# Ten groups of payload scatters moved from the moments stage into the last ticks of the ranking stage of a graph network kernel

## The chip, the cores and the metric

The kernel runs on one core of one Trainium2 chip. The metric is the device time of one execution in microseconds. The kernel before takes 5331.2 us, the median of three runs (5328.56, 5331.2 and 5365.31 us). The execution that the profiler recorded took 5342.85 us, with a profiled span of 5341.1 us.

## The reference

Four graph layers run over 50000 nodes of 128 features and 25000 edges (padded to 25600 = 200 tiles of 128), each inside `x = layernorm(x + layer(x))`. The two stages that matter here belong to the first layer and to the preparation of the second:

```
def _L0_gnn_ref(x, W, b, gamma, beta, edge_index):
    xw = x @ W
    src = jnp.concatenate([edge_index[0], loops]); dst = jnp.concatenate([edge_index[1], loops])
    deg = jax.ops.segment_sum(ones, dst, num_segments=N)
    dinv = jnp.where(deg > 0, jax.lax.rsqrt(deg), 0.0)
    msg = xw[src] * (dinv[src] * dinv[dst])[:, None]
    h = jax.ops.segment_sum(msg, dst, num_segments=N) + b
    mean = jnp.mean(h, axis=0); var = jnp.mean(jnp.square(h - mean), axis=0)
    h = jax.nn.relu((h - mean) * jax.lax.rsqrt(var + BN_EPS) * gamma + beta)
    return x + h
```

The second layer groups edges by their source, `row = edge_index[0]`. The edges come sorted by destination, so the kernel itself works out, for each edge, its place in the order by source (its rank), and writes the edge's record of four integers to that place of a table in DRAM.

## The kernel before, in words

The kernel is a row of stages, each a block of one instruction stream per engine. A stage begins on all engines only when the stage before has ended on all of them. The four stages of interest, in order:

- **Counting** (`count_phase`, L218) makes histograms of the nodes. Beside it GpSimd (POOL) gathers the source rows of `x` for the first FG = 10 groups of edges (`fetch_sources`, L208).
- **Ranking and summing** (`rank_and_sum_phase`, L348) handles T = 200 tiles of 128 edges, in EG = 50 groups of GT = 4 tiles. For each tile VectorE (DVE) makes one-hot rows (`hots`), counts equal sources inside the tile (`twins`, first half of the rank, `parts[:, 0]`) and picks the count of earlier tiles (`picks`, second half, `parts[:, 1]`). TensorE (PE) and ScalarE (ACT) look up tables, weigh the gathered rows and sum them by destination. ACT copies the sums of a tile to `rank_sums`, a ring of US = 3 groups (`copy_sums`), and POOL scatters them to the table `agg` in DRAM. One pass of POOL's `pipeline` is called a tick here: in tick m it gathers the source rows of group m + 10 (four indirect DMAs, L213) while m < 40, and then scatters the sums of group m - 3 (four indirect DMAs, L423), which waits for `copied`. ACT, before it copies a group's sums, waits until the scatter of three groups earlier has landed. After all 200 tiles one DVE instruction adds the two halves to `rank`, an integer table of 128 x 200 (L489).
- **Moments** (`moments_phase`, L1308) goes over the node table in NG + 1 = 49 blocks of 1024 rows: SP loads a block of `x` and of `agg`, DVE combines them in three instructions (L1383, L1388, L1395), PE sums products (L1440, which counts up `used` once a block), SP stores the block. A short chain of small steps on DVE, PE and ACT ends with `gcn_c` (L1421). Beside it POOL runs `send_payloads` (L1501): 50 groups of four indirect DMAs, each of which writes the records of one tile of 128 edges to `sorted4` at their ranks. Group g waits until the payload group two before has landed, and until `used` has reached g - 1.
- **Order by source** (`order_phase` with the tag ord_s, L574) loads `sorted4`, first of all by SP (L593).

POOL's queue is strictly in order: an instruction that waits holds up all behind it.

Of the kernel before, what the change touches and what calls it, by code (L numbers as in the profile page):

```python
# [16 lines left out]
ALU = mybir.AluOpType  # L17
# [9 lines left out]
T = 200  # L27
# [5 lines left out]
GT = 4  # L33
EG = T // GT
# [168 lines left out]


FG = 10


def fetch_sources(k, rows, g):  # L208
# [139 lines left out]
def rank_and_sum_phase(k, order, rows):  # L348

    nc = k.nc  # L350
    with ExitStack() as st:
# [34 lines left out]
        with nc.Block(no_gpsimd_drain=True) as block:  # L386
# [25 lines left out]
            def _(pool):  # L412
                nc.gpsimd.iota(eid[:, :], pattern=[[P, T]], base=0, channel_multiplier=1).then_inc(s["numbered"], 1)

                def gather(g):
                    if g + FG < EG:
                        fetch_sources(k, rows, g + FG)

                def scatter(g):
                    pool.wait_ge(s["copied"], (g + 1) * GT)  # L420
                    for j in range(GT):
                        t = g * GT + j
                        nc.gpsimd.indirect_dma_start(  # L423
                            out=k.agg, out_offset=bass.IndirectOffsetOnAxis(ap=order.last_idx[:, t:t + 1], axis=0),
                            in_=sums[:, g % US, j, :], in_offset=None, bounds_check=N - 1, oob_is_err=False)\
                            .then_inc(k.scattered[g % US], 16)

                pipeline(EG, (gather, 0), (scatter, 3))
                for g in range(EG - US, EG):
                    pool.wait_ge(k.scattered[g % US], stored(g))  # L430

# [1 line left out]
            def _(dve):  # L433
# [49 lines left out]
                    nc.vector.tensor_tensor(cross[:, u, :, :], dst_b[:, u, :, :], prev,  # L483
                                            ALU.is_equal).then_inc(s["masked"], 1)

                pipeline(T, (hots, 0), (twins, 0), (picks, 2), (masks, 2))
                dve.wait_ge(s["twinned"], T)
                dve.wait_ge(s["rank_picked"], T)
                nc.vector.tensor_tensor(rank[:, :], parts[:, 0, :], parts[:, 1, :], ALU.add).then_inc(s["ranked"], 1)  # L489
                dve.wait_ge(s["ranked"], 1)  # L490

            @block.scalar
            def _(act):
# [1004 lines left out]
CS = 4  # L1498


def send_payloads(k, pool, used):  # L1501

    def sent(g):
        return k.scatter_base[RF + g % 2] + g // 2 * 16 * GT + 16 * GT

    for g in range(EG):
        if g >= 2:
            pool.wait_ge(k.scattered[RF + g % 2], sent(g - 2))
            pool.wait_ge(used, min(g - 1, NG + 1))
        for t in range(g * GT, (g + 1) * GT):  # L1510
            k.nc.gpsimd.indirect_dma_start(  # L1511
                out=k.sorted4[:, :], out_offset=bass.IndirectOffsetOnAxis(ap=k.rank[:, t:t + 1], axis=0),
                in_=k.payload[:, t, :], in_offset=None).then_inc(k.scattered[RF + g % 2], 16)
    for g in range(EG - 2, EG):
        pool.wait_ge(k.scattered[RF + g % 2], sent(g))
    for g in range(EG):
        k.scatter_base[RF + g % 2] += 16 * GT

# [1886 lines left out]
```

## Time and profile before

| What | us |
|---|---|
| median of the runs | 5331.2 |
| the profiled execution | 5342.85 |
| its span | 5341.1 |
| busy: PE / DVE / POOL / ACT | 3358.2 / 3813.6 / 3005.8 / 2396.5 |
| ranking stage, first to last scatter of POOL | 191.1 to 684.7 |
| moments stage, first instruction | 687.8 |
| payload scatters of POOL, first and last start | 688.4 and 982.4 |
| first instruction of the order by source | 985.37 |

Times are microseconds from the start of the span unless marked ns. Busy time of an engine is the time in its instructions; register, semaphore and DMA-issuing instructions of the hardware queues are not in it, but POOL's indirect DMAs are, since POOL itself makes their descriptors. The idle time before an instruction is put down to what released it ("issue" means to nothing that the profile shows).

### The profile page before, as it was taken

Reading aid. Unit: us, or ns where it says so; the run is one execution under the profiler, and the core shown is the slowest. Engines: PE = TensorE matmul, PEld = TensorE weight load, DVE = VectorE, ACT = ScalarE, POOL = GpSimd, SP = SyncE. Lnnn points to the kernel's source line nnn. Section 1 sums busy time; section 2 is a strip of 40 time slices with the busy share of each in tenths; the row PEclk is TensorE's granted clock in tenths of the full one; section 3 lists DMA queues with packets and bytes.
Section 4 is the critical chain, followed back from the end, with each engine's and each line's share of the span. In section 5 each row is a group of like instructions: output and inputs, shape, how many; then the busy total and the mean of one; then the engine's idle time right before and its main releaser. Section 6 shows DMA issues by size and latency. Waiting matters only on the chain. (4 is left out here: it accounts for less than half of the span.)

```text
span 5341.1 us, 70175 instructions
## 1 busy us (share of the span) xinstructions
PE 3358.2 (63%) x19808; PEld 2649.4 (50%) x19808; DVE 3813.6 (71%) x10966; ACT 2396.5 (45%) x5571; POOL 3005.8 (56%) x2733
## 2 busy tenths in 40 slices
PE   6888855288612367643277644556999993774453
PEld 1455554277601255533266633334777763764443
DVE  8877777399834467622377777886899874877997
ACT  6444400299700156532123213544666662325776
POOL 7777577245577433257777726765776556107400
PEclk9989977699855689865588867878999996996666
DMA  5666588299757778832367527883555545876654
GB/s 208 180 190 198 167 304 289 92 299 314 242 187 260 249 237 276 275 107 73 96 212 259 186 61 224 279 277 118 182 192 187 178 142 161 264 218 227 232 213 155
DMA packets 684358, 1095.92 MB, mean 205 GB/s; under 512 B 108888, under 2 KB 451979, under 8 KB 677722
## 3 DMA queue, kind: packets, MB, share of 16 engines
q1 hardware_dynamic: 580772, 908.27, 51.9%
q0 software_dynamic: 103200, 183.16, 11.4%
q8 instruction: 162, 2.65, 0.2%
q14 instruction: 224, 1.84, 0.1%
HBM read 664.33 MB, written 439.19 MB: 207 GB/s over the span
## 5 line engine op out<-in xcount | busy, mean ns | idle before, releaser
L2242 PE MATMUL ro_end<-vals,end_mask 128*2 128x128 f32 x1600 | 240.5, 315 | 373.2 <-DVE vals L2106 276.4
L2368 POOL DMA_INDIRECT sc_rows<-layer,node_idx x400 | 391.5, 979 | 124.4 <-issue 121.6
L719 POOL DMA_INDIRECT agg<-late_agg_sent,d_last x200 | 223.2, 1116 | 324.5 <-issue 295.8
L2242 PEld LDWEIGHTS ro_end<-vals,end_mask 128*2 128x2 f32 x1600 | 147.3, 96 | 457.2 <-DVE vals L2106 287.6
L2974 ACT ACTIVATE tf_hidden<-tf_h_ps,pre_b 128x512 f32<-128x512 f32 x392 | 268.8, 687 | 227.0 <-PE tf_h_ps L3014 217.0
L2268 PE MATMUL ro_acc<-vals,ro_mask 128*126 128x128 f32 x1600 | 248.3, 320 | 187.3 <-ACT ro_square L2200 140.5
L1601 POOL DMA_INDIRECT cap_own<-layer,w_own x200 | 205.7, 1028 | 278.9 <-SPq L1581 227.2
L3026 PE MATMUL tf_o_ps<-pre_w,tf_hidden 128*128 128x128 f32 (+1 forms) x3136 | 358.0, 275 | 0.0
L3026 PEld LDWEIGHTS tf_o_ps<-pre_w,tf_hidden 128*128 128x128 f32 (+1 forms) x3136 | 353.9, 192 | 0.5 <-issue 0.5
L3014 PE MATMUL tf_h_ps<-tf_x_t,pre_w 128*128 128x512 f32 x784 | 348.2, 597 | 9.5 <-ACT tf_hidden L2974 8.3
L213 POOL DMA_INDIRECT x_src<-in_x_dram,node_idx x200 | 295.6, 1478 | 81.7 <-issue 59.4
L2056 POOL TENSOR_TENSOR vals<-ro_both,ro_weight 126x1024 f32<-126x1024 f32 x75 | 144.9, 1932 | 341.2 <-ACT ro_weight L2224 300.5
L2268 PEld LDWEIGHTS ro_acc<-vals,ro_mask 128*126 128x126 f32 x1600 | 229.5, 230 | 210.3 <-issue 174.9
L1104 PE MATMUL ml_conv_out<-pre_mean_wt,ml_conv_tsb 128*128 128x128 f32 (+1 forms) x784 | 178.2, 420 | 241.6 <-DVEq L3206 228.7
L791 POOL DMA_INDIRECT msg_rows<-values,s_eid x200 | 206.9, 1034 | 186.5 <-POOLq L71 100.9
L1104 PEld LDWEIGHTS ml_conv_out<-pre_mean_wt,ml_conv_tsb 128*128 128x128 f32 (+1 forms) x784 | 166.4, 322 | 254.0 <-ACT ml_conv_tsb L1090 180.2
L872 PE MATMUL msg_acc<-msg_pair,msg_vals 128*128 128x512 f32 (+3 forms) x400 | 170.8, 587 | 191.9 <-DVE msg_pair L663 167.5
L2875 POOL DMA_INDIRECT tf_edge_x<-y,tf_src_idx x200 | 197.8, 989 | 157.1 <-SPq L2852 99.9
L719 POOL DMA_INDIRECT msum<-late_sent,s_last x200 | 215.6, 1078 | 113.1 <-issue 108.3
L2043 POOL DMA_INDIRECT ro_far<-layer,w_far x200 | 225.6, 1128 | 78.7 <-issue 59.3
L2069 POOL DMA_INDIRECT layer<-ro_far,w_last x200 | 215.3, 1077 | 95.3 <-issue 60.3
L1511 POOL DMA_INDIRECT sorted<-payload,rank x200 | 228.7, 1143 | 68.9 <-issue 63.2
(502 smaller groups left out, 11021.1 us busy)
## 6 DMA issues: line engine op xcount, KB each, us to landing
ro_mask<-masks SPq DMA_DIRECT2D x100, 504.0 KB, 4.9
layer<-zeros SPq DMA_DIRECT2D x96, 512.0 KB
si_both<-layer SPq DMA_DIRECT2D x48, 1024.0 KB, 6.1
ro_far<-far SPq DMA_DIRECT2D x75, 512.0 KB, 6.1
ro_both<-both SPq DMA_DIRECT2D x75, 512.0 KB, 6.0
agg<-zeros SPq DMA_DIRECT2D x48, 512.0 KB
mom_x<-in_x_dram SPq DMA_DIRECT2D x48, 512.0 KB, 9.8
mom_agg<-agg SPq DMA_DIRECT2D x48, 512.0 KB, 8.1
```

What stands on the lines that cost most here:

```text
L213: k.nc.gpsimd.indirect_dma_start(out=rows[:, t, :], out_offset=None, in_=k.x, in_offset=bass.IndirectOffsetOnAxis(ap=k.node_idx[:, 0, t:t ...
L719: pool.indirect_dma_start(out=self.dest, out_offset=bass.IndirectOffsetOnAxis(ap=self.order.last_idx[:, t:t + 1], axis=0), in_=self.sent[: ...
L1104: mm = self.k.nc.tensor.matmul(self.out[b][0:p, j, :], self.turned_sb[:, 4 * b + j, 0:p], self.weight, start=plain, stop=plain or j == 3, ...
L1511: k.nc.gpsimd.indirect_dma_start(out=k.sorted4[:, :], out_offset=bass.IndirectOffsetOnAxis(ap=k.rank[:, t:t + 1], axis=0), in_=k.payload[: ...
L2043: nc.gpsimd.indirect_dma_start(out=far[real, u, j, :], out_offset=None, in_=k.layer1_halves, in_offset=bass.IndirectOffsetOnAxis(ap=wide.f ...
L2069: nc.gpsimd.indirect_dma_start(out=k.layer1_halves, out_offset=bass.IndirectOffsetOnAxis(ap=wide.last[real, t:t + 1], axis=0), in_=sent[re ...
L2242: mm = nc.tensor.matmul(end_ps[0:2, j, :], k.end_mask[:, t, :], k.vals[:, t, :], start=True, stop=True, skip_group_check=True)
L2268: mm = nc.tensor.matmul(acc[w][real, j, :], mask[:, u, j, :], k.vals[:, tile(n, j), :], start=True, stop=True, skip_group_check=True)
L2368: nc.gpsimd.indirect_dma_start(out=rows[:, g % SC, c * GT + j, :], out_offset=None, in_=k.layer1, in_offset=bass.IndirectOffsetOnAxis(ap=k ...
L2974: nc.scalar.activation(hidden[:, h, b, :], h_ps[b][:, :], ACT.Relu, bias=b1[:, b:b + 1]).then_inc(s["bent"], 1)
L3014: nc.tensor.matmul(h_ps[b][:, :], w1[:, b * P:(b + 1) * P], x_t[:, u, 4 * h:4 * h + 4, :].rearrange("p j e -> p (j e)"), start=True, stop= ...
L3026: mm = nc.tensor.matmul(o_ps[h][0:p, j, :], hidden[:, h, b, j * P:j * P + p], w2[:, b, :], start=b == 0, stop=b == NB - 1)
```

## The change

The rank is now added up per group on DVE, three tiles behind the front of its pipeline (`ranks`, 50 instructions of 128 x 4 in place of one of 128 x 200). POOL's pipeline in the ranking stage gets a third step, `payload`: in ticks 40 to 49, which have no gather, it sends the payload scatters of groups 0 to 9 behind the scatter of sums. In the moments stage `send_payloads` sends groups 10 to 49, and the i-th of these 40 groups (i from 1) waits for `used` to reach i * 49 // 40 instead of g - 1.

```
+PG = 10
...
+                def payload(m):
+                    g = m - (EG - PG)
+                    if g >= 0:
+                        pool.wait_ge(s["ranked"], g + 1)
+                        send_payload(k, pool, g)
...
-                pipeline(EG, (gather, 0), (scatter, 3))
+                pipeline(EG, (gather, 0), (scatter, 3), (payload, 0))
...
-                pipeline(T, (hots, 0), (twins, 0), (picks, 2), (masks, 2))
-                dve.wait_ge(s["twinned"], T)
-                dve.wait_ge(s["rank_picked"], T)
-                nc.vector.tensor_tensor(rank[:, :], parts[:, 0, :], parts[:, 1, :], ALU.add).then_inc(s["ranked"], 1)
-                dve.wait_ge(s["ranked"], 1)
+                def ranks(n):
+                    if n % GT != GT - 1:
+                        return
+                    at = slice(n - GT + 1, n + 1)
+                    dve.wait_ge(s["twinned"], n + 1)
+                    dve.wait_ge(s["rank_picked"], n + 1)
+                    nc.vector.tensor_tensor(rank[:, at], parts[:, 0, at], parts[:, 1, at], ALU.add).then_inc(s["ranked"], 1)
+
+                pipeline(T, (hots, 0), (twins, 0), (ranks, 3), (picks, 2), (masks, 2))
+                dve.wait_ge(s["ranked"], EG)
...
+def payload_sent(k, g):
+
+    return k.scatter_base[RF + g % 2] + g // 2 * 16 * GT + 16 * GT
+
+
+def send_payload(k, pool, g):
+
+    if g >= 2:
+        pool.wait_ge(k.scattered[RF + g % 2], payload_sent(k, g - 2))
+    for t in range(g * GT, (g + 1) * GT):
+        k.nc.gpsimd.indirect_dma_start(
+            out=k.sorted4[:, :], out_offset=bass.IndirectOffsetOnAxis(ap=k.rank[:, t:t + 1], axis=0),
+            in_=k.payload[:, t, :], in_offset=None).then_inc(k.scattered[RF + g % 2], 16)
+
+
 def send_payloads(k, pool, used):
...
-    for g in range(EG):
-        if g >= 2:
-            pool.wait_ge(k.scattered[RF + g % 2], sent(g - 2))
-            pool.wait_ge(used, min(g - 1, NG + 1))
...
+    for g in range(PG, EG):
+        if g > PG:
+            pool.wait_ge(used, min((g - PG) * (NG + 1) // (EG - PG), NG + 1))
+        send_payload(k, pool, g)
```

The first place is POOL's queue in the ranking stage where its gathers end (L213 is the gather, L423 the scatter of sums; `rank_copied` is counted up by ACT's copies). Before:

```order
L213 DMA x_src<-in_x_dram,node_idx 128x128 [waits gathered1]
L213 DMA x_src<-in_x_dram,node_idx 128x128 x3
L423 DMA agg<-rank_sums,d_last 50000x128 [waits rank_copied]
L423 DMA agg<-rank_sums,d_last 50000x128 x3
L423 DMA agg<-rank_sums,d_last 50000x128 [waits rank_copied]
L423 DMA agg<-rank_sums,d_last 50000x128 x3
```

And with the change, where L214 is the gather, L430 the scatter of sums and L1523 the payload scatter:

```order
L214 DMA x_src<-in_x_dram,node_idx 128x128 [waits gathered1]
L214 DMA x_src<-in_x_dram,node_idx 128x128 x3
L430 DMA agg<-rank_sums,d_last 50000x128 [waits rank_copied]
L430 DMA agg<-rank_sums,d_last 50000x128 x3
L430 DMA agg<-rank_sums,d_last 50000x128 [waits rank_copied]
L430 DMA agg<-rank_sums,d_last 50000x128 x3
L1523 DMA sorted<-payload,rank 25600x4 [waits rank_ranked]
L1523 DMA sorted<-payload,rank 25600x4 x3
L430 DMA agg<-rank_sums,d_last 50000x128 [waits rank_copied]
L430 DMA agg<-rank_sums,d_last 50000x128 x3
```

Behind the scatters of groups 37 to 46 now stand four payload scatters each; the last three scatters of sums follow one another as before.

The second place is where POOL enters the moments stage (`mom_used` is counted up by PE once a block, `scattered3` and `scattered4` by landed payload groups). Before:

```order
L1364 UNCONDITIONAL_BRANCH [waits barrier_Pool_Activation_PE_DVE_SP_gather]
L1511 DMA sorted<-payload,rank 25600x4 x8
L1511 DMA sorted<-payload,rank 25600x4 [waits mom_used,scattered3]
L1511 DMA sorted<-payload,rank 25600x4 x3
L1511 DMA sorted<-payload,rank 25600x4 [waits mom_used,scattered4]
```

With the change:

```order
L1376 UNCONDITIONAL_BRANCH [waits barrier_Pool_Activation_PE_DVE_SP_gather]
L1523 DMA sorted<-payload,rank 25600x4 [waits scattered3]
L1523 DMA sorted<-payload,rank 25600x4 x3
L1523 DMA sorted<-payload,rank 25600x4 [waits scattered4,mom_used]
L1523 DMA sorted<-payload,rank 25600x4 x3
L1523 DMA sorted<-payload,rank 25600x4 [waits scattered3,mom_used]
```

The first wait for a block now stands before the second group of the stage; before it stood before the third.

The third place is DVE's queue in the ranking stage at the end of a group (L451 is one half of `hots`, L458 `twins`, L466 and L469 `picks`, L482 the first of the `masks`). Before:

```order
L451 TENSOR_SCALAR rank_hot_high<-iota_high,high_col 128x392 [waits rank_dinv_picked,rank_added]
L458 SCALAR_TENSOR_TENSOR rank_twin,rank_parts<-rank_src_b,id_col,earlier 128x128
L466 ISA rank_picked,rank_parts<-rank_look,rank_hot_high 128x392 [waits rank_high_made,rank_looked]
L466 ISA rank_parts 128x1
L469 ISA rank_picked,dinv_src<-rank_look,rank_hot_high 128x392
L469 ISA dinv_src 128x1
L482 TENSOR_TENSOR rank_same<-rank_dst_b,id_col 128x512 [waits rank_dst_ready1]
```

With the change:

```order
L458 TENSOR_SCALAR rank_hot_high<-iota_high,high_col 128x392 [waits rank_dinv_picked,rank_added]
L465 SCALAR_TENSOR_TENSOR rank_twin,rank_parts<-rank_src_b,id_col,earlier 128x128
L499 TENSOR_TENSOR rank<-rank_parts 128x4 [waits rank_rank_picked,rank_twinned]
L473 ISA rank_picked,rank_parts<-rank_look,rank_hot_high 128x392 [waits rank_high_made,rank_looked]
L473 ISA rank_parts 128x1
L476 ISA rank_picked,dinv_src<-rank_look,rank_hot_high 128x392
L476 ISA dinv_src 128x1
L489 TENSOR_TENSOR rank_same<-rank_dst_b,id_col 128x512 [waits rank_dst_ready1]
```

One instruction of 128 x 4 is added per group, between `twins` and `picks`. The picks for which it waits were issued one tile earlier on the same engine.

## Rows read from the trace of the kernel before

**Rows 1.** Windows: busy time (instructions) of each engine in four stretches
```profile
core 0: us, PE busy (x) PEld busy (x) DVE busy (x) ACT busy (x) POOL busy (x), PEclk, DMA share, GB/s
202.00:575.00 373.00, 324.26 (x1452) 209.62 (x1450) 287.20 (x1127) 175.07 (x580) 287.69 (x280) 0.93 0.67 195
593.00:650.00 57.00, 57.00 (x282) 37.78 (x280) 54.68 (x218) 34.41 (x112) 30.94 (x28) 1.00 0.65 184
688.00:924.00 236.00, 136.72 (x789) 125.39 (x789) 192.83 (x209) 2.57 (x3) 183.36 (x154) 0.77 0.97 332
924.00:985.00 61.00, 2.46 (x9) 1.60 (x9) 4.19 (x13) 0.37 (x1) 45.32 (x47) 0.53 0.05 7
```

**Rows 2.** Waits of the stretch 688 to 990, SP's own last: total, times, longest
```profile
POOL sorted L1511 <- issue: 63.2, 193, 4.7
DVE ord_s_minus L609 <- PEq L71: 53.9, 1, 53.9
SPq L1339 <- PEq L1339: 51.9, 1, 51.9
```

**Rows 3.** Timeline, 911 to 990: start, duration, engine, line, operation
```profile
923.68 0.97 POOL L1511 DMA_INDIRECT sorted<-payload,rank  x1 [0.30 <-issue]
...
931.26 0.29 DVE L1421 TENSOR_TENSOR gcn_c<-mom_gb,mom_work 128x128 f32<-128x128 f32 x1
...
936.51 0.97 POOL L1511 DMA_INDIRECT sorted<-payload,rank  x1 [0.30 <-issue]
...
982.37 0.97 POOL L1511 DMA_INDIRECT sorted<-payload,rank  x1 [0.31 <-issue]
985.37 0.30 SPq L593 DMA_DIRECT2D ord_s_row<-sorted  x1
```

**Rows 4.** Groups of POOL, 202 to 575: count, busy us, mean ns, idle
```profile
L423 POOL DMA_INDIRECT agg<-rank_sums,d_last x140 | 145.6, 1040 | 42.7 <-issue 42.7
L213 POOL DMA_INDIRECT x_src<-in_x_dram,node_idx x140 | 142.1, 1015 | 42.7 <-issue 41.8 <-ACT rank_sums L513 0.9
```

**Rows 5.** The scatter of sums from 576 on: what its engine waited for
```profile
  ACT rank_sums L513: 37.3, 11
  issue: 13.9, 45
```

**Rows 6.** Timeline of POOL and of ACT's L513, 574 to 690
```profile
575.28 1.02 POOL L423 DMA_INDIRECT agg<-rank_sums,d_last  x1 [0.30 <-issue]
580.83 1.19 POOL L423 DMA_INDIRECT agg<-rank_sums,d_last  x1 [0.30 <-issue]
584.85 0.28 ACT L513 ACTIVATE rank_sums<-rank_acc 128x128 f32<-128x128 f32 x1 [5.76 <-DMA agg<-rank_sums,d_last]
593.04 1.46 POOL L423 DMA_INDIRECT agg<-rank_sums,d_last  x1 [2.02 <-ACT rank_sums L513]
601.19 1.46 POOL L423 DMA_INDIRECT agg<-rank_sums,d_last  x1 [2.83 <-ACT rank_sums L513]
680.88 0.98 POOL L423 DMA_INDIRECT agg<-rank_sums,d_last  x1 [0.30 <-issue]
684.74 0.98 POOL L423 DMA_INDIRECT agg<-rank_sums,d_last  x1 [0.30 <-issue]
```

**Rows 7.** Groups of POOL, 688 to 924 and 924 to 990
```profile
L1511 POOL DMA_INDIRECT sorted<-payload,rank x154 | 184.0, 1195 | 54.9 <-issue 49.2 <-POOLq L71 2.7 <-PE mom_acc L1440 2.1
L1511 POOL DMA_INDIRECT sorted<-payload,rank x47 | 45.6, 971 | 14.3 <-issue 14.3
```

**Rows 8.** Timeline of POOL at the start of the moments stage
```profile
688.44 0.97 POOL L1511 DMA_INDIRECT sorted<-payload,rank  x1 [2.72 <-POOLq L71]
693.85 0.97 POOL L1511 DMA_INDIRECT sorted<-payload,rank  x1 [0.31 <-issue]
699.78 1.86 POOL L1511 DMA_INDIRECT sorted<-payload,rank  x1 [0.91 <-PE mom_acc L1440]
```

**Rows 9.** Groups of DVE by form, 202 to 575
```profile
L458 DVE SCALAR_TENSOR_TENSOR rank_twin<-rank_src_b,id_col,earlier 128x128 f32<-128x128 f32 x146 | 50.3, 345 | 0.0
L482 DVE TENSOR_TENSOR rank_same<-rank_dst_b,id_col 128x512 f32<-128x512 f32 x36 | 24.8, 689 | 0.0
L483 DVE TENSOR_TENSOR rank_cross<-rank_dst_b,d_prev 128x512 f32<-128x512 f32 x36 | 24.6, 684 | 0.0
L448 DVE TENSOR_TENSOR rank_hot_low<-iota_row,low_col 128x512 f16<-128x512 f16 x36 | 24.6, 684 | 0.0
```

**Rows 10.** Timeline of DVE: the rank's one addition, and a tiny addition elsewhere
```profile
674.24 0.36 DVE L489 TENSOR_TENSOR rank<-rank_parts 128x200 int32<-128x200 f32 x1
847.26 0.15 DVE L1293 TENSOR_TENSOR pre_work<-pre_bc,pre_half 3x8 f32<-3x8 f32 x1
```

**Rows 11.** Payload scatters, 688 to 924: us from issue to landing
```profile
DMA to landing us min/median/max: 3.2/5.6/7.0
```

More of the change, by code:

```diff
@@ L1498 @@
 CS = 4
-def send_payloads(k, pool, used):
-    def sent(g):
-        return k.scatter_base[RF + g % 2] + g // 2 * 16 * GT + 16 * GT
-    for g in range(EG):
-        if g >= 2:
-            pool.wait_ge(k.scattered[RF + g % 2], sent(g - 2))
-            pool.wait_ge(used, min(g - 1, NG + 1))
[L1510 to L1513, printed above, removed]
+def payload_sent(k, g):
[7 more added lines that the diff above has]
+            in_=k.payload[:, t, :], in_offset=None).then_inc(k.scattered[RF + g % 2], 16)
+def send_payloads(k, pool, used):
+    for g in range(PG, EG):
+        if g > PG:
+            pool.wait_ge(used, min((g - PG) * (NG + 1) // (EG - PG), NG + 1))
+        send_payload(k, pool, g)
     for g in range(EG - 2, EG):
-        pool.wait_ge(k.scattered[RF + g % 2], sent(g))
+        pool.wait_ge(k.scattered[RF + g % 2], payload_sent(k, g))
     for g in range(EG):
```

## The prediction, made before the changed kernel ran

> **What bounds the kernel now.** I read the windows by stage first, then the waits and the timeline where two stages meet, then the groups of POOL's instructions. The windows [rows 1] show two stages that POOL alone finishes. In the stretch 924 to 985 PE, DVE and ACT do 2.46, 4.19 and 0.37 us of work in 61 us, and the DMA engines are busy 0.05 of the time: the moments' blocks are through, and POOL sends its last 47 payload scatters one behind another. The timeline [rows 3] gives the edge: the last of the moments' small steps starts at 931.26, POOL's last scatter at 982.37, and the next stage's first load at 985.37. The waits [rows 2] say the same from the other side: DVE had been waiting 53.9 us for that stage and SP 51.9 us, so SP was through at 985.37 - 51.9 = 933.5. And in the moments stage POOL waited for almost nothing but its own issuing (63.2 us in 193 gaps, some 0.3 each). So the end of the moments stage is that of 200 payload scatters.
>
> The ranking stage is POOL's too, but only as long as there are gathers. From 202 to 575 POOL makes 280 requests (140 scatters, 140 gathers) with no wait beyond issuing [rows 4]: (145.6 + 142.1 + 42.7 + 42.7) / 280 = 1.333 us each, 10.66 us for a tick of eight. DVE has 373 - 287.2 = 86 us without work there, PE some 49 [rows 1]. Behind the last gather a tick has four scatters only; POOL catches up and then waits for ACT's copies: 2.83 us in a tick, a tick being 601.19 - 593.04 = 8.15 us, with PE busy all the time, 57.00 of 57.00 us [rows 1, 6]. In all POOL waits 37.3 us for ACT there, 11 times [rows 5].
>
> **The change, part by part.**
>
> *Forty scatters leave the moments stage.* In POOL's lonely tail a scatter costs (45.6 + 14.3) / 47 = 1.274 us [rows 7], so 40 are worth 51.0 us if nothing else changes. Something does: the second group of the stage now waits for the first block, where before the third did. Before, the second group started at 693.85 and the third, released by PE's first block, at 699.78 [rows 8]. With the change the second starts at 699.8, and from there each group stands where the next one stood before. The fortieth and last thus stands in the place of the 41st, whose last scatter (the 164th) started at 936.51, instead of 982.37 [rows 3]: 45.9 us gained. This is still behind SP's 933.5, so POOL keeps the end. The later waits for blocks (up to `used` 47 for the last group, reached well before 924) I take as free, but the cover is thin early on: a block takes 236 / 49 = 4.8 us, so the pace allows a group every 4.8 x 49 / 40 = 5.9 us, and POOL needs 4 x (184.0 + 49.2) / 154 = 6.06 [rows 1, 7]. Uneven blocks may cost some 3 us. Bounds: 51.0 gained if the wait costs nothing (SP's end would allow 51.9), 43 with 3 us of waits. The blocks themselves stay as they are: DMA share 0.97, DVE busy 193 of 236 us, and POOL makes about as many requests beside them as before.
>
> *Forty scatters enter ticks 40 to 49 of the ranking stage.* Here they meet POOL at its limit: 8.15 us of tick against eight requests of at least 1.27 us. The scatter of group 37 opens this part at 580.83, the last scatter of sums starts at 684.74 [rows 6]. With the change come ten ticks of eight requests, then 11 more starts at (684.74 - 680.88) / 3 = 1.287 us, together 14.2. The last scatter starts at 580.83 + 10 T + 14.2. For T, the payload scatter's price beside this stage's work, no row is there. Bounds: the lonely price for payloads and the undisturbed 1.287 for scatters give T = 4 x 1.274 + 4 x 1.287 = 10.24, and a start at 697.4, 12.7 us later than before; the price beside the moments' heavy DVE work, 1.514 [rows 7], with 1.333 for scatters gives T = 11.39, and 24.2 later. I take T = 10.66, since ticks of eight requests beside just this work stand in the trace [rows 4]: 701.6, 16.9 us later. The lower bound has a second source: 40 x 1.274 = 51.0 us of work come in and 37.3 us of waits go out [rows 5], 13.7.
>
> Nobody else should hold this part. ACT's copies of a group wait for the scatter three groups earlier; that loop, with its catch-up, took from the scatter start at 575.28 through ACT's wait until 584.85 to the scatter start at 593.04, 17.8 us [rows 6], and three ticks now take 32.0. The payload groups wait for ranks made many ticks earlier and for payloads two ticks, 21 us, back that land in 7.0 at most [rows 11].
>
> *Fifty small additions on DVE.* The nearest rows are 0.36 us for 128 x 200 and 0.15 for 3 x 8 [rows 10]: 50 x 0.15 = 7.5 us, less the 0.36 of the old one. I price them at nothing: DVE has 86 us of idle time up to 575, and behind that a tick of 10.66 us against 54.68 / 7 = 7.8 of work. Without that cover they would cost 7.
>
> *Sum.* -45.9 + 16.9 = -29.0 us. The profiled execution would go from 5342.85 to 5313.9; it lies 11.7 above the median, and the median would be 5331.2 - 29.0 = 5302. What follows in the program is unchanged, only earlier.
>
> **The rivals.**
>
> *The ring of sums stalls (slower).* If the payloads, which stand between one scatter of sums and the next, delay the landing of the sums, ACT's copies and so PE wait longer. It decides once 10 T exceeds 135.6 us, T = 13.6: then the loop of three ticks lasts 40.7 us instead of 17.8. Were each of four payloads to land before the sums at 7.0 us each, the loop would be 17.8 + 28 = 45.8, T = 15.3, the last scatter at 748, 63.3 later: 5331.2 - 45.9 + 63.3 = 5349. For it: ACT did wait for landed sums in the gather ticks. Against it: it waited because POOL was late, and 23 us of slack stand in between. Chance 0.03.
>
> *DVE holds POOL back.* If each DVE instruction with two operands from SBUF kept a POOL request waiting for its whole length, a tick would grow by 4 x 0.345 + 0.689 + 0.684 + 0.684 = 3.4 us [rows 9] and 0.15 for the new addition: T = 10.24 + 3.6 = 13.8, the last scatter at 733, 48.3 later, in sum +2.4 and 5334. Against it: the gather ticks hold the same DVE instructions and took 10.66, 0.42 above 10.24. For it: beside the moments' DVE work a request is 0.24 longer than alone [rows 7]. Chance 0.05. This is what the Trainium skill, page SBUF — State Buffer, section Who interferes with whom, would lead to: a DVE instruction with two SBUF inputs and a GpSimd instruction that reads SBUF take a shared pair of ports in turns, and the second blocks fully. By that rule the trace agrees in kind (the longer requests), not in size here.
>
> *The payloads are free in the ranking stage.* Were POOL's waits enough, only the gain would be left: 5331.2 - 45.9 = 5285, or 5280 with 51.0. Against it: 37.3 us of waits for 51.0 us of work. It would need requests under 1 us. Chance 0.06.
>
> **How the numbers follow.** The forecast, both stages bound by POOL, has 0.82; 0.04 stay for what I don't name. Its own range is -51.0 + 12.7 = -38.3 to -43 + 24.2 = -18.8: 5293 to 5312. The range given reaches down to the free case's 5285 and up to 5326, for a partial hold-up by DVE and for runs that scatter: 5284 to 5326. About 1%, 53 us, is what a measurement of this kernel can tell from no change. The largest gain of any case, 51.9, falls just short of it, so faster by over 1% gets 0.04 for scatter; slower by over 1% needs more than even the ring gives, 0.03; within 1% gets 0.93.
>
> **What would show it.** Right: POOL without waits for ACT from tick 40 on, ticks near 10.7 us, the moments starting some 17 us later than 687.8, their POOL stretch some 249 us long (688.4 to 937.5 before the shift) instead of 295, and one wait for PE of about 5 us before the second payload group. Wrong in the first part: waits of POOL for ACT in ticks 41 to 49, or the ranking ending within 5 us of before. Wrong in the second: many waits for `used`, or the next stage's first load more than 5 us behind POOL's end. The forecast as a whole falls if the later stages, which I take as unchanged, move by more than 10 us.

## The result, and the profile after

| | before | changed |
|---|---|---|
| median of 8 executions each, us | 5336.7 | 5310.8 |
| lowest to highest, us | 5328.6 to 5365.3 | 5297.6 to 5333.5 |
| the profiled execution, us | 5342.85 | 5303.36 |

The ratio is 0.995, its 95% interval 0.9926 to 0.9975: 25.9 us less in the medians, where the forecast said 29.0. The interval spans 13 to 39 us; it shuts out no change and both slower rivals, and the free case's 45.9 us by a few us. The profiled executions differ by 39.5 us, and I split this by three places of the trace: the ranking stage's first instruction on POOL (an iota, 167.5 before and 160.4 after), the next stage's first load (985.37 [rows 3], now 947.01), and the end. Up to the iota 7.1 us are gone, in a stage that the change does not touch; the section on the hardware shows what varies there. From the iota to the load it took 817.9 us and now takes 786.6: 31.3 less, and this is the change's own effect in the profile. The rest took 4355.7 and takes 4354.6.

The windows of the changed kernel: stretch, its length, then busy time and instructions of each engine, the granted clock of PE, the DMA share and GB/s. They answer to [rows 1]; the second is the ten ticks that payloads have entered.

```profile
core 0: us, PE busy (x) PEld busy (x) DVE busy (x) ACT busy (x) POOL busy (x), PEclk, DMA share, GB/s
195.00:568.00 373.00, 325.17 (x1451) 209.44 (x1450) 289.84 (x1161) 175.05 (x581) 287.32 (x281) 0.93 0.68 195
573.00:681.00 108.00, 90.24 (x397) 58.65 (x396) 75.09 (x301) 47.88 (x160) 83.01 (x83) 0.91 0.45 129
697.00:935.00 238.00, 133.08 (x789) 121.94 (x789) 192.46 (x209) 2.77 (x3) 178.44 (x153) 0.78 0.97 329
935.00:947.00 12.00, 2.62 (x10) 1.60 (x9) 4.16 (x13) 0.37 (x1) 6.80 (x7) 0.64 0.14 32
```

The first row is that of before almost to the instruction (281 requests of POOL in 373 us, 280 before). The stretch in which the other engines had nothing to do was 61 us long and is 12.

The groups of POOL in 573 to 681 (the first two) and 697 to 935 (the third): count, busy us, mean ns, then the idle time and what ended it. They answer to [rows 5] and [rows 7].

```profile
L430 POOL DMA_INDIRECT agg<-rank_sums,d_last x43 | 43.8, 1019 | 13.1 <-issue 12.8 <-ACT rank_sums L525 0.3
L1523 POOL DMA_INDIRECT sorted<-payload,rank x40 | 41.4, 1036 | 12.2 <-issue 12.2
...
L1523 POOL DMA_INDIRECT sorted<-payload,rank x153 | 178.4, 1166 | 61.5 <-issue 46.4 <-PE mom_acc L1452 8.6 <-DMA sorted<-payload,rank 3.5
```

POOL's 37.3 us of waits for ACT are gone: the one wait of 0.3 us that is left is as long as the gap that stands between any two of its requests ([0.30 <-issue] in the timeline). POOL now issues one request behind another through the ranking's end. The timeline of the changed kernel (start, duration, engine, line, operation, idle time before), at the edges of the two stretches:

```profile
573.35 0.98 POOL L430 DMA_INDIRECT agg<-rank_sums,d_last  x1 [0.30 <-issue]
...
679.59 1.00 POOL L430 DMA_INDIRECT agg<-rank_sums,d_last  x1 [0.30 <-ACT rank_sums L525]
...
693.77 0.98 POOL L430 DMA_INDIRECT agg<-rank_sums,d_last  x1 [0.30 <-issue]
697.87 0.97 POOL L1523 DMA_INDIRECT sorted<-payload,rank  x1 [3.11 <-POOLq L71]
...
709.72 1.79 POOL L1523 DMA_INDIRECT sorted<-payload,rank  x1 [7.06 <-PE mom_acc L1452]
...
942.51 0.29 DVE L1433 TENSOR_TENSOR gcn_c<-mom_gb,mom_work 128x128 f32<-128x128 f32 x1
942.71 0.97 POOL L1523 DMA_INDIRECT sorted<-payload,rank  x1 [0.30 <-issue]
947.01 0.30 SPq L605 DMA_DIRECT2D ord_s_row<-sorted  x1
```

573.35 and 679.59 are the first scatters of the ticks of groups 37 and 47: ten ticks in 106.24 us, 10.62 us each, against 8.15 before and 10.66 in the forecast. 697.87 is the first payload scatter of the moments stage, 942.71 the last: 244.8 us for 160, where 200 took 293.9 [rows 3, 8]. SP's own waits in 930 to 948:

```profile
SPq L1374 <- DMA y<-mom_y: 12.0, 2, 10.9
...
SPq L1351 <- PEq L1351: 2.1, 1, 2.1
```

SP was through at 947.01 - 2.1 = 944.9, 1.2 us after POOL's last request ended (943.68). Before, POOL's end (983.34) lay 49.8 us behind SP's (933.5). But POOL does not leave the stage with its last request: it waits at L1535 until the last payloads have landed. That wait was over at 946.1 (duration in ns, then first and last start):

```profile
L1535 POOLq EVENT_SEMAPHORE  x1: 17/17/17, 946.1 to 946.1; - x1
```

SP's wait of 2.1 us is the wait for the others to leave the stage. So POOL still ended the stage, with SP some 1.2 us ahead of it.

### The profile page after: what moved, and what is told of

The parts are those of the page before. It is cut to its first block and busy times, and to the rows that moved or that the text cites. A ratio compares the mean times of both kernels' runs of the same rounds, so it can differ in the third digit from the quotient of the medians.

```text
span 5301.6 us, 70169 instructions
## 1 busy us (share of the span) xinstructions
PE 3349.1 (63%) x19705; PEld 2653.7 (50%) x19808; DVE 3815.1 (72%) x11015; ACT 2395.0 (45%) x5571; POOL 3000.9 (57%) x2733
## 5 line engine op out<-in xcount | busy, mean ns | idle before, releaser
L214 POOL DMA_INDIRECT x_src<-in_x_dram,node_idx x200 | 288.9, 1445 | 81.6 <-issue 59.7
L1523 POOL DMA_INDIRECT sorted<-payload,rank x200 | 226.7, 1133 | 75.9 <-issue 60.7
```

The lines of the kernel that those rows point to most:

```text
L214: k.nc.gpsimd.indirect_dma_start(out=rows[:, t, :], out_offset=None, in_=k.x, in_offset=bass.IndirectOffsetOnAxis(ap=k.node_idx[:, 0, t:t ...
L1523: k.nc.gpsimd.indirect_dma_start(out=k.sorted4[:, :], out_offset=bass.IndirectOffsetOnAxis(ap=k.rank[:, t:t + 1], axis=0), in_=k.payload[: ...
```

## The experiments

One table first, worked out from the profile of each kernel. "Ranking" is from the iota to the start of the last scatter of sums, "moments" from that stage's first load to the next stage's, "payloads" the starts of the first and the last payload scatter within it and how many, "blocks" the time from the stage's first load to `gcn_c`, the last small step behind its blocks.

| kernel | iota | ranking | moments | payloads | blocks | iota to next stage | after it |
|---|---|---|---|---|---|---|---|
| before | 167.5 | 517.2 | 297.6 | 293.9 (200) | 243.5 | 817.9 | 4355.7 |
| before again | 157.8 | 514.0 | 299.3 | 295.6 (200) | 242.2 | 816.4 | 4352.4 |
| changed | 160.4 | 533.4 | 249.8 | 244.8 (160) | 245.3 | 786.6 | 4354.6 |
| ranks only | 158.4 | 518.7 | 300.5 | 296.8 (200) | 238.3 | 822.7 | 4360.4 |
| seven groups | 158.3 | 515.8 | 268.2 | 264.6 (172) | 241.7 | 787.5 | 4358.2 |
| old pace | 161.1 | 533.5 | 246.5 | 242.8 (160) | 244.2 | 783.4 | 4351.8 |
| thirteen groups | 158.6 | 550.3 | 238.8 | 235.1 (148) | 236.4 | 792.5 | 4356.1 |
| by one, 24 ahead, 14 | 167.9 | 502.9 | 241.4 | 225.1 (144) | 239.8 | 747.7 | 4355.9 |

The kernel before, profiled a second time, gives the scatter of these columns between two executions: 3 us in the ranking, 2 in the moments, 3 behind them, and 10 ahead of the iota. The ratios below are each to executions of the kernel before on the same chip.

**Ranks per group, no payload moved.**

```
-PG = 10
+PG = 0
-                pipeline(EG, (gather, 0), (scatter, 3), (payload, 0))
+                pipeline(EG, (gather, 0), (scatter, 3))
-            pool.wait_ge(used, min((g - PG) * (NG + 1) // (EG - PG), NG + 1))
+        if g >= 2:
+            pool.wait_ge(used, min(g - 1, NG + 1))
```

> Only one part of the change: the rank is added up per group (50 additions of 128 x 4 on DVE), all 50 payload groups stay in the moments stage with the pace of before. My theory (DVE is covered): from the start of the scatter of sums of group 37 to that of the last scatter of sums 104 us as before (103.9), POOL's payload stretch in the moments stage 294 us, ratio to before within 0.2% of 1. Rival (the additions cost): 50 x 0.156 = 7.8 us more in the ranking stage, ratio 1.0015.

Measured: a ratio to before of 1.0009 (0.9999 to 1.0018, 10 and 13 executions). The groups of POOL in 566 to 683, and below it one line of the changed kernel, the fifty additions (count, then min, median and max ns, first and last start):

```profile
L430 POOL DMA_INDIRECT agg<-rank_sums,d_last x56 | 59.1, 1056 | 53.3 <-ACT rank_sums L525 39.1 <-issue 14.2
```

```profile
L499 DVE TENSOR_TENSOR rank<-rank_parts x50: 150/156/229, 174.2 to 670.4; 128x4 int32<-128x4 f32 x50
```

The additions are 0.156 us each, and POOL's wait for ACT is back at 39.1 us. What they cost is within the scatter: the last scatter of sums starts 105.9 us after that of group 37, where the two profiles of the kernel before have 103.9 and 101.6, and the ranking took 518.7 us for 517.2 and 514.0. The interval of the ratio alone would not shut out the rival's 1.0015; the profile shows less than its 7.8 us. The change's gain comes from where the forty payload scatters stand.

**The kernel before once more**, to have a second profile beside the others.

> The kernel before once more, for the scatter between executions. In the two profiled executions so far the ranking stage began at 167.5 us (before) and at 158 to 161 us (the changed kernel and four variants), with 18 and 30 gathers done when one gather in the counting stage stood still for 71.5 to 74 us. If that difference is chance (my theory), this execution may fall anywhere from 158 to 168; if the change causes it, it falls at 167 to 168 with 18 gathers again.

One execution: 5328.4 us. Its row in the table says what differs without any edit: the iota came at 157.8, so the 7 us ahead of the iota are chance and no effect of the change.

**Seven groups early instead of ten** (`PG = 7`; the pace is computed from it).

> Seven payload groups in the ranking stage instead of ten (ticks 43 to 49), 43 in the moments stage. Theory one (POOL bounds both places): the seven ticks of eight requests take 10.66 us each from the scatter of group 40 at 601.2 on (times of the kernel before), so the last scatter of sums starts at 690, 5.3 us later than before, and the payload stretch of the moments stage is 244.8 + 12 x 1.274 = 260 us; in all 28 to 29 us less than before, 2 to 3 more than with ten groups. Theory two (payloads are free in the ranking stage while POOL has waits left): the last scatter of sums as before, 34 us less than before.

Measured: 0.993 (0.9913 to 0.9947, 4 executions). The groups of POOL in 563 to 680:

```profile
L430 POOL DMA_INDIRECT agg<-rank_sums,d_last x56 | 57.6, 1028 | 17.1 <-issue 16.5 <-ACT rank_sums L525 0.6
L1523 POOL DMA_INDIRECT sorted<-payload,rank x30 | 30.8, 1027 | 12.0 <-issue 8.5 <-POOLq L71 3.1 <-ACT rank_sums L525 0.3
```

The ranking took 515.8 us, and the last scatter of sums started 105.6 us after that of group 37; the three profiles without payloads there have 514.0 to 518.7 and 101.6 to 105.9. So seven groups entered the ranking for nothing that can be told from the scatter. My reading had been that they would cost 5 us, since part of the 37.3 us [rows 5] lay in ticks 41 and 42 and would be lost; it fell. The row says where it went: POOL's waits for ACT are three of 0.3 us, the ordinary gap between two requests, so every one of the 37.3 us was filled. 28 scatters at the lonely 1.274 us are 35.7 us, just under 37.3. The moments then took 18.4 us longer than with ten groups, and the whole is within 1 us of the changed kernel (787.5 and 786.6). Groups 8 to 10 cost 533.4 - 515.8 = 17.6 us in the whole ranking, of which 120.4 - 105.6 = 14.8 stand behind group 37, where they were added (12 scatters at 1.23), and bring 18.4 in the moments. Within the scatter that is break-even.

**The old pace for the forty groups left.**

```
-        if g > PG:
-            pool.wait_ge(used, min((g - PG) * (NG + 1) // (EG - PG), NG + 1))
+        if g > PG + 1:
+            pool.wait_ge(used, g - PG - 1)
```

> The changed kernel with the first wait for a block moved back by one group: the third group of the moments stage waits for the first block, every later one for one block more. Theory one (POOL alone ends the moments stage, as I forecast): POOL ends some 8 us earlier in the stage (7.06 us of wait for the first block, and the few later ones), and the next stage begins 6 to 8 us earlier. Theory two (POOL now ends together with the others: last scatter 942.71, last small step of DVE 942.51, SP's last wait over at 944.9, next stage at 947.0): POOL ends earlier, but the next stage begins at most 2 us earlier, 248 us or more after the stage's first load instead of 249.8.

Measured: 0.9931 (0.991 to 0.9953, 4 executions), which can't be told from the changed kernel's 0.995. In the waits of 690 to 950 POOL stands so:

```profile
POOL sorted L1523 <- PE mom_acc L1452: 2.4, 8, 0.3
```

No wait is longer than 0.3 us, the ordinary gap, so the wait of 7.06 us is gone; and the moments took 246.5 us instead of 249.8. Half of what was saved came out at the end of the stage, between what the two theories said. POOL still ended the stage. The 160 scatters themselves took more time here (from the first scatter of the stage on, count, busy us and mean ns, with the changed kernel first):

```profile
L1523 POOL DMA_INDIRECT sorted<-payload,rank x160 | 185.2, 1158 | 63.7 <-issue 48.5 <-PE mom_acc L1452 8.6 <-DMA sorted<-payload,rank 3.5
```

```profile
L1523 POOL DMA_INDIRECT sorted<-payload,rank x160 | 189.2, 1182 | 57.7 <-issue 49.4 <-POOLq L71 3.1 <-DMA sorted<-payload,rank 2.7
```

That is 4.0 us more, and a single gap of POOL, which every kernel has some 180 us into this stage and which the profile puts down to nothing, was 6.3 us long for 5.0. Why the scatters differ by 2% is open. Here the next load (944.5) follows the last payload scatter (941.5) by 3.0 us, as in the kernel before; in the changed kernel by 4.3. The spreading of the forty groups brings nothing; it costs 0 to 3 us.

**Thirteen groups early** (`PG = 13`).

> Thirteen payload groups in the ranking stage, three of them in ticks 37 to 39, which have gathers too. Both theories: the ranking stage grows by 12 x 1.333 = 16 us against the changed kernel, since POOL has no idle time in it. Theory one (POOL ends the moments stage): 12 scatters less there give 15.3 us back, in all within 2 us of the changed kernel. Theory two (blocks, stores and small steps end it): at most 2 us come back, in all 14 to 16 us slower than the changed kernel, some 12 us faster than before.

Measured: 0.994 (0.9923 to 0.9958, 4 executions). Two rows, the scatter of sums and the payload scatter (min, median, max ns, first and last start), and SP's first load of the next stage:

```profile
L430 POOL DMA_INDIRECT agg<-rank_sums,d_last x200: 982/997/1534, 182.9 to 708.9; - x100
```

```profile
L1523 POOL DMA_INDIRECT sorted<-payload,rank x200: 965/972/2025, 552.2 to 948.1; - x100
```

```profile
L605 SPq DMA_DIRECT2D ord_s_row<-sorted x1: 303/303/303, 951.1 to 951.1; - x1
```

The ranking got 16.9 us longer, as expected: from the eighth group on, twelve scatters cost some 17 us there, 1.4 each. The moments got 11.0 shorter. How much the moments would give back is where the theories differed, and neither is met exactly. The payload scatters still ended it (951.1 follows 948.1 by 3.0), but the blocks themselves were through after 236.4 us instead of 245.3. Over the kernels of the table their length varied from 236 to 245 without following the number of payloads beside them (238.3 with 200, 245.3 with 160, 236.4 with 148). So the floor is about 240 and itself moves by some 4 either way; what it moves with is open. The 148 scatters left took 1.225 us each in the mean, for 1.158 with 160 and 1.182 with the old pace, so POOL got back less than it gave away.

**Where else POOL's requests could go.** In the ranking each group of gathers that is sent earlier makes room. The kernel sends ten groups ahead, in the counting stage (`FG = 10`), and one gather there can take very long (last section). These kernels try to make that stage usable. First the comparisons of `cnt_hot_high` with a source in rows of 8 at a pitch of 10, nothing else:

```
+        high_rows = k.sb(st, "cnt_high_rows", [P, NG + 1, NJ + 2], FP16)
-                        nc.vector.tensor_scalar(hot_high[:, n % 4, a, :], k.iota_high16[:, :],
+                        nc.vector.tensor_scalar(hot_high[:, n % 4, a, :].rearrange("p (c j) -> p c j", j=NJ),
+                                                high_rows[:, :, 0:NJ],
```

> The changed kernel, with the one-hot rows of the counting stage (16-bit comparison of 128 x 392) reading their counter from a table of 49 rows of 8 at a pitch of 10. Nothing else differs, and the values are the same. Theory one (DVE's comparison, in the form that it has now, keeps POOL from making descriptors while it runs back to back, and this layout takes it out of that form): no gather of the counting stage lasts over 3 us, all 40 are done by 80 us instead of at 160, the comparisons get longer (some 0.26 us apart instead of 0.24, the stage's DVE work 5 to 15 us longer), and the ranking stage begins at about the same time as now, 155 to 170. Theory two (the stand-still is the queue's or the DMA engines'): one gather of about 70 us stays.

Measured: a median of 5341.8 us over 10 executions (one of them at 7575.7, for which I have no cause), ratio 1.001 (1.0 to 1.002) to before. No gather of the counting stage took over 1.452 us. But the comparisons got slower by more than expected, the iota moved from 160.4 to 193.6 where 155 to 170 was expected, and the 26 us of the change were gone. The same with 24 groups ahead (`FG = 24`):

> As p1_rows, with the gathers of 24 groups instead of 10 in the counting stage, so the ranking stage has gathers in ticks 0 to 25 only. If POOL is free in the counting stage, 96 gathers of 1.25 us take 120 us there and end at about 145 to 155. The ranking stage then loses 56 requests of 1.333 us, but its ticks without gathers are at best 8.15 us: ticks 26 to 39 save 14 x 2.5 = 35 us. Theory one: some 35 us less from the start of the ranking stage to its last scatter than the changed kernel's 533, the total 20 to 35 us below the changed kernel. Theory two (POOL stays locked out): the gathers are only made later, the total 10 to 60 us above it.

Measured: 0.9941 (0.9925 to 0.9958), 5306.1 us. 14 groups of gathers, 56 requests, left the ranking, and it took 496.3 us, 37.1 less than in the changed kernel, of 35 expected. It paid back the 33 us of slower comparisons and no more. With 14 groups of payloads early and the old pace (`PG = 14`) besides:

> As p2, with 14 payload groups in the ranking stage (ticks 36 to 49) instead of 10 and the pace in the moments stage as in e4. POOL has 2.8 us a tick without gathers to spare over 24 ticks, 68 us, and 14 groups are 56 requests of 1.333 us, 75 us. Theory one (POOL's idle time in the ranking stage is what carries payloads for nothing, as e3 showed for seven groups): the ranking stage some 7 us longer than p2's at most, the moments stage at 236 to 240 us as in e5, the total 5 to 10 us below p2. Theory two (the moments stage doesn't get shorter): the total at or above p2.

Measured: 0.9956 (0.9939 to 0.9972), 5308.3 us; ranking 503.8 us, moments 241.0. Against the kernel above, 16 more scatters cost 7.5 us in the ranking and brought 12.5 in the moments, 5 us in the profiles that the times do not show.

**Smaller comparisons of `cnt_hot_low` between them.** Instead of one 128x512 comparison for four columns, one 128x256 for two of them:

```
+                LW = 2
-                    each = k.low_col16[:, g * GT:(g + 1) * GT].unsqueeze(2).broadcast_to([P, GT, P])
+                    each = k.low_col16[:, n:n + LW].unsqueeze(2).broadcast_to([P, LW, P])
...
-                    lows(g)
-                    for n in range(g * GT, (g + 1) * GT):
-                        highs(n)
+                for n in range(T):
+                    if n % LW == 0:
+                        lows(n)
+                    highs(n)
```

> The changed kernel, with the low one-hot rows of the counting stage (DVE, 128 x 512, the only instruction there that lets POOL through) made two tiles at a time: two instructions of 128 x 256 with four high comparisons between them in place of one of 128 x 512 with eight. Theory one (each such instruction is a window for one POOL request): gathers 1.2 to 1.3 us apart instead of 2.45 once the stage runs, all 40 done by about 75 us, no stand-still; DVE's part of the stage 3 us longer, the ranking stage from about 160. Theory two (a window must be 0.68 us long): POOL stands still for most of the stage, and the ranking stage begins at 185 to 200.

Measured: 0.9958 (0.9943 to 0.9973, 10 executions), the changed kernel's time. Neither theory holds: one gather stood for 91.18 us, and yet the iota came at 169.6. Then one comparison for each column (`LW = 1`), with `FG = 24`, `PG = 14` and the old pace:

> Low rows of the counting stage one tile at a time, gathers of 24 groups there, 14 payload groups in the ranking stage, pace as in e4. Theory one (short windows are enough): 96 gathers end by 150 us, the ranking stage begins at about 168 (DVE's counting part 8 us longer) and takes 504 us as in p3, the moments stage 241: next stage at 168 + 504 + 3 + 241 = 916, 30 us earlier than in the changed kernel, total about 5275. Theory two (POOL is locked out for good): counting ends at 250 us or later, total 5340 or more.

Measured: **0.9893 (0.987 to 0.9915)**, 5276.0 us (5272.5 to 5281.2, 4 executions), which beats the kernel before and the changed one. Its scatter of sums, and what POOL waited for there:

```profile
L434 POOL DMA_INDIRECT agg<-rank_sums,d_last x200: 982/992/1494, 191.6 to 670.8; - x100
its engine sat idle before it (us, times) until:
  issue: 59.0, 188
  ACT rank_sums L529: 24.2, 11
```

The iota came 7.5 us later than in the changed kernel (167.9 for 160.4), the ranking took 30.5 less and the moments 8.4 less; from the iota to the next stage it is 747.7 us for 786.6. POOL waits for ACT again, 24.2 us in all. By the profile more payloads there should bring nothing, though this was not tried: in this kernel the moments no longer end with POOL, whose last payload scatter starts 15.6 us ahead of the next stage, but with the blocks (239.8 us of 241.4). What the small comparisons themselves are worth was not shown: a kernel with 24 groups ahead and the comparisons of before was not run, and in three profiles POOL went through the counting stage beside these freely (last section). A middle way, `LW = 2`, `FG = 20`, `PG = 12`:

> Low rows two tiles at a time, gathers of 20 groups in the counting stage, 12 payload groups in the ranking stage, pace as in e4. Theory one: 80 gathers end by 150 us, the ranking stage begins at about 160 and takes some 508 us, the moments stage 243, next stage at 914, total 5270 to 5280. Theory two: counting ends at 230 us or later, total 5330 or more.

Measured: 0.9993 (0.9976 to 1.0011, 10 executions). One gather stood for 93.69 us, 80 gathers had to be out before the ranking, and the iota waited until 222.3, near what the second theory says.

## Why the prediction held, point by point

**The ticks of the ranking's end.** Right in mechanism and size. T is 10.62 us for 10.66, the last scatter starts 120.4 us after that of group 37 where it was 103.9 [rows 6], 16.5 later for 16.9. POOL's row shows requests of 1.02 and 1.04 us with 0.3 between, and no waiting for ACT beyond such a gap: the engine is bound by its own requests, as in the gather ticks [rows 4].

**The ring of sums** did not stall. ACT waited for landed sums in the same ticks, and more than before (5.8 us in one wait from 580 to 690),

```profile
ACT rank_sums L525 <- DMA agg<-rank_sums,d_last: 24.5, 8, 5.9
```

but POOL did not wait for ACT: the slack between them took it, as the forecast had it.

**DVE holding POOL back** would have given T = 13.8; it was 10.62. In this stage the rival falls. In the counting stage POOL is held in some executions, beside another kind of DVE instruction, below.

**Payloads free in the ranking.** Wrong as a whole, right for seven tenths. The forecast had both numbers, 37.3 us of waits and 1.274 us a scatter [rows 5, 7], and used them only as the difference for forty, a bound that it did not take. Divided they say that 29 scatters, seven groups, go in for nothing, and the run with seven shows it. The three last groups then cost 14.8 us where they stand, for 12 x 1.274 = 15.3. The sum for ten comes out the same either way.

**The fifty additions.** 0.156 us each; no cost beyond the scatter of 2 to 4 us: right as far as the runs can tell.

**The moments.** The forecast took 45.9 us off POOL's stretch; 49.1 came off (293.9 to 244.8). The first wait for a block was 7.06 us where "about 5" were expected, but that figure did not follow from the forecast's own rows: they put the second group 699.8 - 688.44 = 11.4 us behind the first, and it came 709.72 - 697.87 = 11.9 behind. The later waits, which I took as free, were free: the profile lists five, 1.5 us together, and each is the ordinary gap of 0.3. What was off is the price of a scatter, 1.166 us in the mean for 1.195 [rows 7], 4.4 us over 153; that this price came out lower is luck: over the whole stage it was 1.158 here, 1.182 with the old pace and 1.225 with thirteen groups early. **POOL keeps the end** held, though closer than forecast: SP's last store was through 247.7 us after the stage's first load instead of 245.7, and POOL's last payloads landed 2.4 us behind its last request (943.68 to 946.1). The next stage therefore followed the last scatter by 4.3 us, not 3.0. In sum the moments gave 47.8 for 45.9: 49.1 less the 1.3 of the late landing.

**The sum**: -47.8 + 16.5 = -31.3 us between the iota and the next stage, against -29.0; the later stages moved by 1.1. The medians say -25.9, with an interval of the ratio that spans 13 to 39 us. So the executions confirm the direction and the rough size; that the parts are the forecast's is what the profiles show.

## What to carry to other kernels

When an engine's lonely tail is to be filled into another stage, divide the waits that it has there by the price of one request: so many are free (here 37.3 / 1.274 = 29 of 40), and each one beyond costs what it brings. So the last third of the change brought no more than it cost (14.8 to 17.6 us for 18.4), and three groups more cost 16.9 us and brought 11.0. Then look at who ends the emptied stage next; here the blocks and SP's stores stood within a few us of POOL, and in the last kernels, with 144 and 152 payloads beside them, they ended the stage. Further gain lay in a stage where the same engine had time that its busy share did not show.

## What the runs showed of the hardware

In the counting stage DVE runs the `cnt_hot_high` comparisons back to back, 128x392 of 16-bit numbers with one operand from SBUF, and POOL gathers beside it. The timeline of POOL in the kernel before:

```profile
75.33 71.54 POOL L213 DMA_INDIRECT x_src<-in_x_dram,node_idx  x1 [0.30 <-issue]
147.18 0.94 POOL L213 DMA_INDIRECT x_src<-in_x_dram,node_idx  x1 [0.30 <-issue]
```

One gather lasts 71.54 us, until DVE's counting loop is done, and the next 0.94. In the changed kernel one at 73.22 lasts 74.00; in the second profile of before none lasts over 2.156. The iota waits for the gathers that are left, which is the 10 us of scatter ahead of the ranking. DVE in that second profile (DVE, then POOL):

```profile
74.93 0.69 DVE L259 TENSOR_TENSOR cnt_hot_low<-iota_row,low_col 128x512 f16<-128x512 f16 x1
75.53 1.94 DVE L267 TENSOR_SCALAR cnt_hot_high<-iota_high,high_col 128x392 f16<-128x392 f16 x8
77.38 0.68 DVE L259 TENSOR_TENSOR cnt_hot_low<-iota_row,low_col 128x512 f16<-128x512 f16 x1
```

```profile
75.44 2.15 POOL L213 DMA_INDIRECT x_src<-in_x_dram,node_idx  x1 [0.30 <-issue]
77.89 2.15 POOL L213 DMA_INDIRECT x_src<-in_x_dram,node_idx  x1 [0.30 <-issue]
```

A gather ends 0.2 us after a two-operand comparison has begun (77.59 and 77.38), and the next ends one whole period of 2.45 us later: it seems as if it could finish only while that comparison runs, not during the eight others, and the expectation for the kernel with pairs of columns above takes it so. But the same two instructions of DVE do not always hold POOL. In the kernel with ranks only, whose counting stage is the same, DVE and POOL stand so:

```profile
55.51 0.68 DVE L260 TENSOR_TENSOR cnt_hot_low<-iota_row,low_col 128x512 f16<-128x512 f16 x1
56.11 1.98 DVE L268 TENSOR_SCALAR cnt_hot_high<-iota_high,high_col 128x392 f16<-128x392 f16 x8
58.01 0.68 DVE L260 TENSOR_TENSOR cnt_hot_low<-iota_row,low_col 128x512 f16<-128x512 f16 x1
```

```profile
56.55 0.95 POOL L214 DMA_INDIRECT x_src<-in_x_dram,node_idx  x1 [0.30 <-issue]
57.80 0.94 POOL L214 DMA_INDIRECT x_src<-in_x_dram,node_idx  x1 [0.30 <-issue]
```

The gather at 56.55 begins and ends within the eight one-operand comparisons, at its undisturbed 0.95 us. All 40 gathers of that stage are so (22 to 147, ranks only):

```profile
L214 POOL DMA_INDIRECT x_src<-in_x_dram,node_idx x40 | 38.2, 954 | 32.9 <-POOLq L71 21.0 <-issue 11.9
```

The kernel with seven groups shows the same (963 ns), and so does most of the one with thirteen (1034 ns). So with these comparisons POOL is in one of three states. It runs free, a gather every 1.25 us, and then DVE's period is 2.50 us; it gets one gather through in a period, which is then 2.45 us; or a single gather stands until DVE's loop ends, which three of seven profiles show. The profiles of the changed kernel and of the old pace pass through all three in this order. What leads from one state to the next is open. The counting stage is the same program in all seven, so it may be where POOL's request falls against DVE's instructions; this was not tested.

With the source in rows at a pitch of 10, DVE takes longer over the comparison and POOL is free; DVE by form in 30 to 140, and POOL in 22 to 147 (count, busy us, mean ns):

```profile
L270 DVE TENSOR_SCALAR cnt_hot_high<-cnt_high_rows,high_col 128x392 f16<-128x392 f16 x278 | 93.1, 405 | 0.0
```

```profile
L214 POOL DMA_INDIRECT x_src<-in_x_dram,node_idx x40 | 39.7, 993 | 32.7 <-POOLq L71 20.8 <-issue 11.9
```

405 ns for 318, and 993 ns a gather for 1936, in the second profile of the kernel before. Of the 232 gathers in the three kernels with this layout none took over 1.5 us. It fits this that the fast form of the one-operand comparison is what shuts POOL out when it is shut out. But it is not shown: with the fast form, too, three profiles of seven had nearly no hold. The Trainium skill, page SBUF — State Buffer, section Who interferes with whom, says that a one-source instruction in a 2-port mode contends with GpSimd for a shared pair of ports, that whichever issues first has the pair for the whole instruction and the other blocks fully, and, marked there as inferred, that a two-source one leaves the making of descriptors alone. The Trainium skill, page Vector Engine (DVE) Microarchitecture Reference, section 5.1 Performance modes, makes that mode depend on the outermost dimension being even, or odd with source and destination of the same size; a source in 49 rows beside a destination in one piece would be neither, but no run shows in which mode DVE was. The traces with a held gather agree with the first of these in kind, and those with free gathers beside the same comparisons do not: there nothing blocks fully, and the measurement decides. How long a single request can stand the traces show by themselves: 71.5 to 93.7 us. With one small two-operand comparison for each column POOL gets through regularly, in the kernel with 24 groups ahead:

```profile
74.34 1.02 POOL L214 DMA_INDIRECT x_src<-in_x_dram,node_idx  x1 [0.30 <-issue]
75.67 1.03 POOL L214 DMA_INDIRECT x_src<-in_x_dram,node_idx  x1 [0.30 <-issue]
```

```profile
75.80 0.55 DVE L271 TENSOR_SCALAR cnt_hot_high<-iota_high,high_col 128x392 f16<-128x392 f16 x2
76.26 0.28 DVE L263 TENSOR_TENSOR cnt_hot_low<-iota_row,low_col 128x128 f16<-128x128 f16 x1
76.46 0.55 DVE L271 TENSOR_SCALAR cnt_hot_high<-iota_high,high_col 128x392 f16<-128x392 f16 x2
76.92 0.28 DVE L263 TENSOR_TENSOR cnt_hot_low<-iota_row,low_col 128x128 f16<-128x128 f16 x1
```

A two-operand comparison of 0.28 us every 0.66, and a gather every 1.33 us, two periods; the price is DVE's counting loop 10 us longer (what follows it starts at 156.8 for 146.8). With one of 0.43 us every 1.26 us, one gather stood again:

```profile
58.99 91.18 POOL L214 DMA_INDIRECT x_src<-in_x_dram,node_idx  x1 [0.31 <-issue]
150.47 0.94 POOL L214 DMA_INDIRECT x_src<-in_x_dram,node_idx  x1 [0.30 <-issue]
```

Which of these rhythms hold for certain and which let a gather stand is open: the kernel before did both. In the one with a small comparison in each column no gather stood long in any of its four executions, by their times (5272.5 to 5281.2), but only one of them has a profile.
